# Last step of two row normalisations on GpSimd instead of VectorE

## The reference

```
def _ln(x):
    m = jnp.mean(x, axis=-1, keepdims=True)
    v = jnp.var(x, axis=-1, keepdims=True)
    return (x - m) / jnp.sqrt(v + EPS)
x = _ln(src) * (1.0 + scale) + shift                 # ahead of attention
...                                                  # q, k, v, 16 heads with a bias of their own, softmax
x = x + (ctx @ Wo + bo)
h = _ln(x) * g2 + beta2                              # ahead of feed-forward
ff = _gelu2(h @ W1 + b1) @ W2 + b2
return x + ff
```

## Time and profile before

| | |
|---|---|
| median of 3 runs | 924.31 us (923.58 to 925.27) |
| profiled execution | 923.14 us, span of the core 921.1 us |
| TensorE busy | 859.3 us, 93% (5712 matmuls) |
| VectorE busy | 740.4 us, 80% (2371 instructions) |
| ScalarE busy | 729.5 us, 79% (1904) |
| GpSimd busy | 236.6 us, 26% (236) |
| HBM traffic over the span | 141 GB/s |

### The profile page before, as it was taken

How to read it: one execution, slowest core, us unless ns; L and a number is a source line. 1 busy time by engine, 2 the same in 40 slices (tenths; PEclk the granted TensorE clock), 3 DMA queues, 4 the chain that set the end, 5 groups by cost and what they waited for, 6 DMA issues and landing times.

```text
span 921.1 us, 18266 instructions
## 1 busy us (share of the span) xinstructions
PE 859.3 (93%) x5712; PEld 665.7 (72%) x5797; DVE 740.4 (80%) x2371; ACT 729.5 (79%) x1904; POOL 236.6 (26%) x236
## 2 busy tenths in 40 slices
PE   9876979999999999999999999999999999999987
PEld 8564657777777777777777777777777777777666
DVE  8767798888898888788898898788898898865542
ACT  2134879889798879979798878979798888977763
POOL 2232223332222313332123323232132323120000
PEclk9996999999999999999999999999999999999999
DMA  9827473744456453744446462744446452646400
GB/s 258 237 69 185 142 192 93 196 121 117 136 155 164 134 156 98 208 122 125 138 143 157 137 166 82 194 143 138 133 131 172 118 165 91 189 133 168 142 12 23
DMA packets 133082, 130.90 MB, mean 142 GB/s; under 512 B 18265, under 2 KB 123481, under 8 KB 132969
## 3 DMA queue, kind: packets, MB, share of 16 engines
q1 hardware_dynamic: 101616, 112.02, 42.9%
q10 hardware_dynamic: 31370, 17.71, 6.9%
HBM read 112.61 MB, written 17.07 MB: 141 GB/s over the span
## 4 chain that ended last, share of the span: by engine, by line
PE 57%; ACT 20%; DVE 8%; issue 3%; POOL 0%; ACTq 0%; DVEq 0%
PE ff_ps L1368 11%; PE ff_ps L1349 8%; PE PT_ps L1404 7%; ACT Pr L1083 5%; PE G L1154 5%; PE scores_ps L1389 4%; PE G L1146 4%; PE ctx_ps L1426 3%; DVE bias L928 3%; ACT L1083 3%; PE scores_ps L1386 2%; ACT ffT L1069 2%; ACT tanh L1065 2%; PE ff_ps L1335 2%; ACT PT L1096 2%
## 5 line engine op out<-in xcount | busy, mean ns | idle before, releaser
L1083 ACT ACTIVATE Pr<-bias,nmax 128x256 f32<-128x256 f32 x512 | 255.8, 506 | 35.3 <-DVE nmax L928 34.6
L928 DVE CUSTOM_DVE_ANT_0 bias<-scores_ps,bias 128x256 f32<-128x256 f32 x512 | 194.0, 419 | 48.2 <-PE scores_ps L1389 26.7
L1096 ACT ACTIVATE PT<-PT_ps 128x512 f32<-128x512 f32 x256 | 152.4, 596 | 50.9 <-PE PT_ps L1404 46.3
L1404 PE MATMUL PT_ps<-ident,Pr 128*128 128x128 f32 x1024 | 156.0, 274 | 7.8 <-ACT Pr L1083 7.8
L566 POOL TENSOR_TENSOR rstd<-var,half_neg 128x2 f32<-128x2 f32 (+1 forms) x64 | 43.4, 678 | 388.6 <-DVE var L691 244.5
L1404 PEld LDWEIGHTS PT_ps<-ident,Pr 128*128 128x128 f32 x1024 | 119.9, 141 | 16.6 <-ACT Pr L1083 13.0
L1349 PE MATMUL ff_ps<-ctxT,w 128*128 128x256 f32 x480 | 117.2, 387 | 13.0 <-ACT ffT L1069 10.7
L1368 PE MATMUL ff_ps<-w,ffT 128*128 128x256 f32 x480 | 113.1, 381 | 0.3 <-DVE ffT L905 0.3
L1349 PEld LDWEIGHTS ff_ps<-ctxT,w 128*128 128x128 f32 x480 | 86.3, 190 | 33.0 <-ACT ffT L1069 16.3
L1389 PE MATMUL scores_ps<-k_stack,q_stack 96*128 96x256 bf16 x512 | 99.3, 275 | 6.1 <-issue 2.1
L1083 ACT ACTIVATION_READ_ACCUMULATOR Pr<-bias,nmax 128x1 f32 x512 | 100.5, 196 | 0.0
(11 more groups left out here) (223 smaller groups left out, 1649.0 us busy)
## 6 DMA issues: line engine op xcount, KB each, us to landing
bias<-in_fside_Bx16xSxS_dram SPq DMA_DIRECT2D x256, 256.0 KB, 3.2
part_dram<-front ACTq DMA_DIRECT2D x32, 384.0 KB, 2.8
q_stack<-part_dram SPq DMA_DIRECT2D x32, 192.0 KB, 3.8
k_stack<-part_dram SPq DMA_DIRECT2D x32, 192.0 KB, 3.7
F<-in_x_dram SPq DMA_DIRECT2D x16, 256.0 KB, 3.7
ada<-rows_dram SPq DMA_DIRECT2D x16, 256.0 KB, 4.6
q_stack<-part_dram SPq DMA_DIRECT2D x32, 128.0 KB, 3.7
k_stack<-part_dram SPq DMA_DIRECT2D x32, 128.0 KB, 3.7
```

The lines of the kernel that those rows point to most:

```text
L928: nc.vector.tensor_tensor_reduce(out=t, in0=SP_[:, n % 2, q * S:(q + 1) * S], in1=t, scale=-1.0, scalar=BIG, op0=ALU.add, op1=ALU.min, acc ...
L1083: ins = nc.scalar.activation(Pr[:, n % PR, q, :], bias[:, n // CH % RING, 2 * (n % CH) + q, :], ACT.Exp, bias=nmax[:, n, q:q + 1], scale=-1.0,
L1096: nc.scalar.activation(PT[:, m % BATCH, :, :].rearrange("p c q -> p (c q)"), TP[:, m % 2, :], ACT.Identity).then_inc(pt_ok, 1)
L1404: ins = pe.transpose(TP[:, m % 2, c * S + q * P:c * S + (q + 1) * P], Pr[:, m % PR, q, c * P:(c + 1) * P], ident[:, :])
```

## The change

In GpSimd's queue the pair of tensor_scalar instructions of `xn3` follows directly behind `inv3` (the same slots), and that of `hn`, under the new name `hn_p`, behind `inv5`. VectorE keeps `hn` for the very last sequence alone. The formula, the buffers and the semaphores signalled are the same; the two new steps wait for GpSimd's own inverse deviation.

In the tables, `AT["xn3"]` goes from (22.25, 37) to (20.5, 44.5), the slots of `inv3`, and `AT_FIRST["xn3"]` from (20.5, 37.75) to (20.25, 43.5), its slots in turn 0. `hn_p` is new: (21.75, 47.25) in `AT` and (33.75, 45) in `AT_LAST`, the slots of `inv5`. In the queues (lines added are GpSimd's up to the last "...", and VectorE's below it):

```diff
+            def row_norm(dst, src, m, r):
+
+                for t in range(src.shape[1]):
+                    ins = nc.gpsimd.tensor_scalar(dst[:, t, :], src[:, t, :], m[:, t, 0:1], r[:, t:t + 1],
+                                                  ALU.subtract, ALU.mult)
+                return ins
...
                 for b in seqs("inv3", j, n):
                     inv(b, 2, 3)
+                for b in seqs("xn3", j, n):
+                    pool.wait_ge(rstd_ok[b], 4 * j + 4)
+                    row_norm(xn3[b], x3[b], mv[:, 2 * b:2 * b + 2, :], rstd[:, b, :]).then_inc(xn3_ok, 1)
...
+                for b in seqs("hn_p", j, n):
+                    if ends(j, b):
+                        continue
+                    half = slice(2 * b, 2 * b + 2)
+                    pool.wait_ge(back_rstd_ok, 2 * j + b + 1)
+                    row_norm(ffT[:, 0:2, :], x5[:, half, :], back_mv[:, half, :], back_rstd[:, half, 0]).then_inc(hn_ok, 1)
...
-                for b in seqs("xn3", j, n):
-                    mine = slice(2 * b, 2 * b + 2)
-                    dve.wait_ge(rstd_ok[b], 4 * j + 4)
-                    row_norm(xn3[b], x3[b], mv[:, mine, :], rstd[:, b, :]).then_inc(xn3_ok, 1)
-
                 for b in seqs("hn", j, n):
+                    if not ends(j, b):
+                        continue
                     half = slice(2 * b, 2 * b + 2)
                     dve.wait_ge(back_rstd_ok, 2 * j + b + 1)
-                    row_norm(ff_at(j, b)[:, 0:2, :], x5[:, half, :], back_mv[:, half, :], back_rstd[:, half, 0]).then_inc(hn_ok, 1)
+                    row_norm(end_ffT[:, 0:2, :], x5[:, half, :], back_mv[:, half, :], back_rstd[:, half, 0]).then_inc(hn_ok, 1)
```

More of the change, by code:

```diff
@@ L85 @@
       "aff1": (18, 34), "y1": (18.5, 33.75), "w_out": (19, 35.75), "x3": (20, 36.5), "inv3": (20.5, 44.5),
[1 row of a table removed]
[1 row of a table added]
       "q_split": (25.5, 40.25), "q_out": (25.25, 42), "k": (25.5, 41), "kf": (25, 40.5), "k_split": (26.75, 41.75),
[L88 to L95, removed]
[7 rows of a table removed]
+      "k_out": (28, 41.75), "v": (28.75, 46), "V": (29, 46.5), "mask": (20, 2), "hn_p": (21.75, 47.25)}
+AT_FIRST = {"s_gelu": (3.25, 3.25), "s_sin": (0.25, 0.25), "s_se": (2.75, 2.75), "s_trig": (3.5, 3.5),
+            "s_onehot": (4, 4), "s_grid": (4.25, 4.25), "s_h1": (3, 3), "s_h2": (3.5, 3.5), "s_h2t": (3.75, 3.75),
+            "s_sel": (2, 2), "s_cond": (4.5, 4.5), "s_condt": (6.25, 6.25), "s_mask": (24.25, 24.25),
+            "s_rows": (15.25, 15.25), "x4": (28, 46.75), "s_fill": (4.25, 4.25), "s_bq": (7.75, 7.75),
+            "s_w2": (34.25, 34.25), "prods_p": (0.25, 5.5), "prods": (5.5, 6), "diffs": (5.5, 6.5),
[8 rows of a table added]
+            "q_out": (28, 40.75), "k": (22.5, 40.75), "kf": (28, 40.5), "k_split": (22.25, 41), "k_out": (29, 42.75),
+            "v": (28.5, 43.25), "V": (25.75, 44)}
 AT_LAST = {"ctx_spread": (23.25, 35.25), "ctx": (20.5, 41.25), "ctx_scale": (20.5, 38.5), "wo": (22, 46),
@@ L107 @@
            "ff": ((24.25, 26.5, 29.5, 30.5), (54.5, 54.5, 58.25, 65)),
-           "w2": ((31.25, 37, 47, 48.25), (67, 73.25, 75.75, 77.5)), "out": (55.25, 70), "store": (57, 68.75)}
+           "w2": ((31.25, 37, 47, 48.25), (67, 73.25, 75.75, 77.5)), "out": (55.25, 70), "store": (57, 68.75),
+           "hn_p": (33.75, 45)}
 SP_AT = {"front": (0, 7), "stacks": (1, 2, 9, 11), "mask": 6, "rows": (12, 3)}
```

## The result

The changed kernel takes 945.68 us (median of 4 runs, 944.6 to 947.25) where the kernel before, on the same chip, took 923.94 (921.9 to 925.27, 4 runs). The ratio is 1.0237, 95% interval [1.0212, 1.0262]: 21.7 us slower. I had forecast 930.5, range 922 to 936. The direction was right, the size was outside the range. The profiled execution took 944.83 us (span 943.0). Lines of the changed kernel are numbered anew: GpSimd's row_norm is L568, its inverse deviation L575, VectorE's variance step L684, the transposes of the norms L1149.

The account below looks back on a forecast made before the run. The prediction took TensorE, 93% busy, to bound the kernel. First sequences 4.6 us plus first and last turns 1.6 us, with nothing for second sequences or VectorE's relief, made 924.3 + 6.2 = 930.5 us, range 922 to 936.

Parts of the forecast that it names:

- What bounds the kernel: Whole kernel: TensorE, busy 93% of the span, with under 2 us in 50 to give back in steady turns.
- relief counted as nothing: VectorE: losing 62 norm instructions, 29.8 us busy, gains no time because nothing on the path needs it.
- the rival at 919.7: Steady turns: VectorE's chain sets the turn; with cheap instructions 0.65 us return seven times, 4.6 us; chance 0.15.
- The price, 0.75 us from half the mask row: GpSimd's 128x256 norm instruction: half its 1.50 us 128x512 mask instruction, so a pair takes 1.50 us against VectorE's 0.73.
- 1.50 as a bound: GpSimd's norm instruction: upper bound, the whole 128x512 mask instruction, if per-partition scalars and a second operation cost as much again.
- a cheap case: GpSimd's norm instruction takes 0.3 to 0.6 us; total 925 at 0.45 us, 927.5 at 0.6; chance 0.20.
- Step 1: First sequence, turns 1 to 7: res1 holds back_var, delaying maxima, exponentials and TensorE 0.66 us, seven times, 4.6 us.
- back_var slips past: First sequence: VectorE's back_var falls between GpSimd's instructions; late norm costs 0.65 to 0.85 us a turn; counted with forecast.
- Step 2: Second sequence: costs nothing; x1 finishes 0.3 us late within 0.32 us slack, feed-forward norm has 0.6 us cover.
- Step 3: First and last turns, norm on the path: +0.35, -0.2, and 0.73 paid twice, sum 1.6 us.
- The dear-instruction rival: GpSimd's instruction takes over 1 us, making the feed-forward norm late; at 1.1 us 938; chance 0.07.
- What would show it wrong: Changed profile: turn within 104.6 us at 0.75 us price, TensorE waiting directly for steady feed-forward norms, or span under 921.

Follow-up runs that it names:

- 0.87 us: Changed kernel with GpSimd's norm cut to 144 of 256 columns, giving instructions of 867 and 897 ns: 932.06 us (1.0091).
- attention-only kernel: Changed kernel with only the attention norm on GpSimd, the feed-forward norm back on VectorE: 945.33 us (ratio 1.0229).
- holding x4 back: Attention norm alone on GpSimd, plus a wait: the first sequence's first x4 follows VectorE's feed-forward norm in turns 1 to 7: 931.89 us (1.0082).
- the version with the late norm: Changed kernel with feed-forward norm on VectorE; first sequence's attention norm on GpSimd behind the feed-forward inverse deviation, turns 1 to 7: 928.32 us (1.0052).
- the control: Kernel before, only the first sequence's two x4 products moved behind the next inverse deviation in GpSimd's queue: 931.69 us (1.0088).

## Why the prediction was wrong, point by point

- **What bounds the kernel, and relief counted as nothing:** right. With GpSimd's norm at 2 columns, and no norm on VectorE but the last, the ratio is 0.999 [0.9977, 1.0004]; the rival at 919.7 is out. That VectorE would lose some 30 us was wrong: 11.2.
- **The price, 0.75 us from half the mask row: wrong, and the step that failed.** It is 1.23 to 1.26. The mask row has other types and one operation with an immediate, and halving it halves the fixed 0.38 us too. I had 1.50 as a bound and then gave all above 1 us a chance of 0.07 and cut the range at 936. The bound called for more. The Trainium skill (GPSIMD Engine Reference, 3.1 Elementwise) has 1.03 cycles per element for a loop of at most two operations, and I had weighed it as a cheap case; the columns measured here, 3.3 ns each where the prediction's estimate by the Trainium skill has 0.22 us for 256, do not agree, and the second operation costs 0.22 us by itself.
- **Step 1, 0.66 us by way of back_var, maxima and exponentials: a wrong path.** At 1.23 us back_var slips past, at 362.36, while the pair's second instruction runs, and keeps its 0.17 us. At 0.87 us it is held, as I had said, and the exponentials do not care. What reaches TensorE in both is the other branch, that I had put among the rivals: the norm itself late. I had read the order of rows at 357.60 as a dependence on the maximum just before it, without showing that this exponential used that one.
- **Step 2, nothing at the second sequence:** right for 0.75 (with 0.87 us there is no wait), and with its cover of 0.6 us nearly right at the dear price too: 411.92 + 2.46 = 414.38, some 0.4 late by its own rows, 0.62 measured, with a pair of 2.59 us. Wrong was that x1 would be held until GpSimd's first instruction ends: in the changed kernel x1 (412.09, 0.91 us against 0.75 before) ends at 413.00, GpSimd's instruction only at 413.13.
- **Step 3, the ends:** the right places; 1.4 + 1.8 + 1.8 instead of 1.6 in all, by the price. Of the 1.4 us of turn 0, 0.95 was left at the first feed-forward norm. The 1.5 us of lower clock in the last turn stood in no term of mine.
- **The dear-instruction rival** gives the result if it is run at 1.23: res1 ends at 355.05 + 2.46 + 1.27 = 358.78, the inverse at 359.6, the norm at 362.1, TensorE 2 us late, seven times 13 to 14; second sequences 3; ends 5: 945 to 946. The mechanism was at hand; the weight was on the wrong price.
- **What would show it wrong** named a wait of TensorE directly for the feed-forward norm in the steady turns. It is the row with 18.5 us. The turn is 106.9 us, not 105.3.

The attention-only kernel's turn is longer than its 2.0 us wait explains: 107.35 us in the mean, from the transposes at 154.49 to those at 798.57, against 104.6. Much of the excess is the clock. Three of its six turns take 107.8 us, and in each of these the granted clock behind the 2.0 us wait is 0.66 in the mean of five us (154 to 159, 475 to 480, 690 to 695), while at 262, 368 and 583 us it is 1.00; the other three take 106.6 to 107.1. So a part of that kernel's 21 us, and of the 13.4 us that holding x4 back saved, is the lower clock.

Left open: an exponential 25 us behind the norm comes 0.3 us later in some turns of the attention-only kernel, in the version with the late norm and in the control, and I did not take it apart. Nor was the hold of the variance step in the changed kernel (1.13 us at 367.75) tried by itself; the two waits of a turn already make up more than its 2.3 us.

## What to carry to other kernels

Price an instruction by a fixed part and a part per column, from two sizes of the same operation count and types; where the trace has no such row, let the range reach the bound. An instruction moved to another engine is paid by what stands behind it in that queue, so follow that queue to the first consumer of TensorE, and check of each link that this reader uses that result. A time that comes out right does not show that the path was right. And look at what the moved work pushes: a two-input GpSimd instruction has to land where VectorE does something that it does not hold.

## What the runs showed of the hardware

- **GpSimd's tensor_tensor holds VectorE's tensor_scalar to its end:** 128x2 took 1.13, 0.82 and 1.34 us instead of 0.17; 128x256 in pairs 2.69 instead of 0.73; SCALAR_TENSOR_TENSOR pairs with inputs in SBUF 2.33 instead of 0.88. VectorE's bias_and_max, with scores from PSUM, is never held: its 512 instructions take 0.41 to 0.43 us in the changed kernel.
- **GpSimd's own tensor_scalar hardly does:** back_var 0.17 us in the middle of it, the norm 0.98 instead of 0.73. Beside VectorE's two-input tensor_tensor both get longer, 1.38 us instead of 1.22 on GpSimd and 0.92 instead of 0.69 on VectorE. The Trainium skill (SBUF — State Buffer, Who interferes with whom) has the second to issue fully blocked until the first finishes when VectorE is in a two-port mode. By that rule the norm at 360.37 would have waited for the whole first instruction of 1.23 us, until 361.56; it had done both of its own by 361.35. No trace here shows in which mode the norm runs. For VectorE's tensor_scalar beside GpSimd's tensor_tensor the traces agree with the Trainium skill.
- **A GpSimd tensor_scalar of 2 columns takes 0.38 to 0.46 us**, so splitting one in two costs that much again: four of 128 columns are 3.2 us, two of 256 are 2.4.
